# Gated cross-attention block on one Trainium2 core: fewer row maxima ahead of the first step, more inside group 0, and weight rounding 23 steps later

## The chip, the cores and the metric

One NeuronCore of one Trainium2 chip. The time is device microseconds for one launch of the kernel, the median of several runs.

## What is computed

The reference takes `x` (4 batches, 512 rows, 512 columns) and a context of 4 x 1601 x 512:

```python
x = x + tanh(g_xattn[0]) * attention(layernorm(x), ctx_2048, ctx_2048)   # 16 heads of 32, scores / sqrt(32)
x = x + tanh(g_ffn[0]) * ffn(layernorm(x))     # fp8-quantised weights and rows, I = 1408
# attention: scores masked to -10000 where key > query + (1601 - 512), softmax over keys, times values
# ffn: each weight row scaled by max|row| / 448 and rounded to fp8 e4m3, likewise each row of x and of the hidden layer
```

The softmax subtracts a shift that is the row maximum of the scores, so each head's scores are made twice: once (queries as rows) for the maxima and once (keys as rows) for the exponentials.

## The kernel before, in words

The work is 16 groups (`GALL`): 4 batches x 4 groups of 4 heads. A group is 26 **steps** (`STEPS` = 2 head pairs x 13 tiles of 128 keys), and every engine runs the same loop `for at in range(END)` with `gg, u = divmod(at, STEPS)`; what an engine does in a step is written out by hand. There is one queue of instructions for each engine, in order, and semaphores between them.

In each step of group `gg`:

- PE makes one **maximum job** (`max_turn`, L777: two matmuls of K = 32 into a slot of two PSUM banks, plus mask matmuls L782 on the diagonal) for a later group, then the two heads' scores (`scores`, L839), then the value product of two steps earlier (`values`, L863).
- DVE reduces the maximum job (`max_reduce`, L1066) out of its slot. There are two slots (banks 4-5 and 6-7), taken in turn by all short PSUM jobs: maximum, stage, suffix, shift, turned output and weight. PE waits for a slot until its job before last has been taken out.
- ACT makes the exponentials (`exps`, L629).

A group has 26 maximum jobs: 13 for its first head pair, 13 for its second. In each 13, the fifth to the eighth are narrower ones. Before, all 26 jobs of group 0 and the first 6 (`AHEAD`) of group 1 run before step 0; from then on there is one a step, always 6 steps ahead (`max_job_at`). After the last job of a group DVE makes `m16` (`max_finish`, L1068 to L1077), PE turns it (`shift_turn`, L791), ACT copies it to `mrow` (L605), and SP's queue sends it by DMA into the last row of `qst` (`put_shift`, L340). `scores` waits for that row (`mrow_in`) at step 0 of its group.

Each group's keys and queries are turned and split into high and low halves two groups ahead (`stage_turn` L764/L756, `stage_high` L589, `stage_low` L1057), and SP's queue copies them into `kst` and `qst` with 24 DMAs a group (`put_heads`, L335/L336).

The **SP queue** also issues nearly all loads, in program order. Ahead of step 0: `x`, keys of group 0, gates, index, keys of group 1, value tiles 0 to 2, the 24 `put_heads` DMAs of group 0, value tiles 3 to 12 (`load_values`, L321), `put_shift(0)` (L340), two down-weight loads (L326), keys of group 2, `put_heads` of group 1.

The **weights** are quantised in 26 jobs: 4 of 1408 columns (down weights, 7 steps apart), 22 of 512 (3 steps apart), starting at `weight_base(j)`. A job is DVE statistics (L996 to L1000), ACT scaling (L559, L562), DVE exponent, rounder and add (L978, L982, L986), a POOL subtraction (L416), PE transposes (L917, L919) and ACT copies (L570 to L577). The first row tile of the FFN starts at step 119 (`tile_base(0)`).

Every group also has three stage jobs at steps 10, 13, 19, a suffix job (L805 to L810, DVE L1082) at step 8, two outputs (`out_turn` L820, `join_out` L1096 to L1109) at steps 4 and 17, `max_finish` at step 20, and the shift at step 23. Every fourth group loads the next batch's values.

## Time and profile before

| what | before |
|---|---|
| median of 3 runs | 1157.04 us (1155.66 to 1158.47) |
| the profiled execution's own time | 1155.15 us |
| its span | 1153.4 us |
| PE busy | 969.0 us (84%) |
| DVE busy | 862.0 us (75%) |
| ACT busy | 656.3 us (57%) |
| POOL busy | 312.9 us (27%) |
| mean granted TensorE clock | 0.952 |

The profiled execution is 1.9 us below the median. Busy shares are averages over the whole span; for this change the stretch before the first scores and the groups 0 to 4 matter, so they are read by time below.

### The profile page before, as it was taken

The page shows a single profiled execution, that of the slowest core. Times are in us where ns is not written, and L with a number is a line of the kernel's source. Part 1 is how long each engine was busy: PE and PEld are TensorE (multiplying, and loading weights), DVE is VectorE, ACT ScalarE, POOL GpSimd, SP SyncE. Part 2 cuts the span into 40 slices and gives each one's busy share as a digit, 9 for nine tenths or more (in the row PEclk, how much of TensorE's full clock was granted, in tenths as well). Part 3 has the DMA queues.
Part 4 walks back from the last instruction along what each step waited for, and adds up shares of the span by engine and source line. Part 5 has one row for each costly group of instructions (what it writes and reads, how often), then busy time and mean ns, then how long its engine had stood idle before and what let it go on. Part 6 is the DMA issues. An engine that isn't in the chain of part 4 may idle for free.

```text
span 1153.4 us, 21093 instructions
## 1 busy us (share of the span) xinstructions
PE 969.0 (84%) x7770; PEld 399.7 (35%) x7770; DVE 862.0 (75%) x1450; ACT 656.3 (57%) x1343; POOL 312.9 (27%) x338
## 2 busy tenths in 40 slices
PE   4588889888879989999889999999889999983444
PEld 2233333333323333333334333333334343442222
DVE  7768789887747887777687878787778777436775
ACT  2165567676636666666556666666566666763322
POOL 3012334332101423232322232232323232433212
PEclk9998899999989999999999999999899999995766
DMA  7942423231572212124822221108621020000000
GB/s 149 159 118 67 117 67 94 66 78 35 103 98 53 71 47 49 44 53 71 125 46 63 67 55 41 48 24 128 81 56 40 20 48 11 2 10 10 10 10 19
DMA packets 155119, 70.69 MB, mean 61 GB/s; under 512 B 111032, under 2 KB 142856, under 8 KB 155016
## 3 DMA queue, kind: packets, MB, share of 16 engines
q1 hardware_dynamic: 153256, 63.57, 26.8%
q0 software_dynamic: 1760, 5.77, 1.8%
q8 instruction: 62, 1.02, 0.4%
q14 instruction: 41, 0.34, 0.1%
HBM read 39.08 MB, written 4.19 MB: 38 GB/s over the span
## 4 chain that ended last, share of the span: by engine, by line
PE 42%; DVE 38%; issue 11%; ACT 4%; POOL 3%; DMA 1%; SPq 0%; POOLq 0%; DVEq 0%; ACTq 0%
DVE mch L1066 18%; PE ps L863 12%; PE ps L839 8%; PE ps L884 6%; PE ps L777 5%; PE ps L907 3%; DVE ff L982 2%; DVE ff L978 2%; DVE ff L986 2%; PE ps L782 2%; ACT pr L629 1%; DVE upd L1109 1%; DMA qst<-mrow 1%; DVE cmb L1099 1%; PE ps L845 1%
## 5 line engine op out<-in xcount | busy, mean ns | idle before, releaser
L629 ACT ACTIVATE pr<-ps 128x512 f32<-128x512 f32 (+4 forms) x832 | 397.1, 530 | 247.0 <-PE ps L839 125.8
L1066 DVE TENSOR_REDUCE mch<-ps 128x2 f32<-128x1024 f32 (+4 forms) x416 | 432.0, 1055 | 68.2 <-PE ps L777 32.8
L863 PE MATMUL ps<-pr,vf 128*33 128x512 f32 (+4 forms) x1664 | 379.8, 536 | 0.0
L839 PE MATMUL ps<-qst,kst 97*64 97x512 f16 (+4 forms) x1600 | 250.6, 371 | 17.7 <-DMA qst<-mrow 11.2
L777 PE MATMUL ps<-kTh,qTh 32*128 32x512 f16 (+4 forms) x832 | 156.0, 373 | 60.0 <-DVE mch L1066 40.9
L777 PEld LDWEIGHTS ps<-kTh,qTh 32*128 32x128 f16 x832 | 39.5, 91 | 277.9 <-DVE mch L1066 106.9
L839 PEld LDWEIGHTS ps<-qst,kst 97*64 97x64 f16 (+1 forms) x1600 | 77.3, 111 | 107.3 <-ACT pr L629 57.1
L863 PEld LDWEIGHTS ps<-pr,vf 128*33 128x33 f32 (+1 forms) x1664 | 86.9, 113 | 57.1 <-issue 5.5
L1142 DVE SCALAR_TENSOR_TENSOR ff<-ps,scs,wsb 128x352 f32<-128x352 f32 x56 | 32.6, 583 | 71.3 <-PE ps L884 71.2
L884 PE MATMUL ps<-wgu,t_T 128*64 128x352 bf16 x768 | 66.5, 316 | 0.0
L445 POOL TENSOR_TENSOR t_q<-ff 128x768 bf16<-128x768 f32 (+1 forms) x24 | 40.4, 1682 | 87.5 <-DVE ff L986 87.5
L429 POOL TENSOR_TENSOR ff<-ff,wsb 128x352 f32<-128x352 f32 x48 | 45.9, 957 | 64.6 <-DVE ff L1142 64.6
L1057 DVE TENSOR_TENSOR kTl<-ps,kTh 128x1024 f16<-128x1024 f32 (+1 forms) x32 | 31.6, 991 | 40.7 <-ACT kTh L589 40.7
L845 PE MATMUL ps<-maskT,idb 128*64 128x128 bf16 (+2 forms) x576 | 61.4, 213 | 0.0
L450 POOL TENSOR_TENSOR xs<-xs,ff 128x512 f32<-128x512 f32 x14 | 17.8, 1272 | 143.9 <-DVE ff L1186 143.9
L986 DVE TENSOR_TENSOR ff<-ff 128x512 f32<-128x512 f32 (+3 forms) x66 | 55.0, 833 | 2.1
L656 ACT ACTIVATE ff<-ps,scs 128x352 f32<-128x352 f32 x48 | 26.6, 553 | 52.2 <-PE ps L884 52.2
L884 PEld LDWEIGHTS ps<-wgu,t_T 128*64 128x64 bf16 x768 | 44.4, 111 | 32.6 <-issue 20.8
L457 POOL TENSOR_TENSOR xs<-xs,upd 128x256 f32<-128x256 f32 x32 | 23.9, 748 | 107.9 <-DVE upd L1109 107.9
L433 POOL TENSOR_TENSOR ff<-ff 128x352 f32<-128x352 f32 x48 | 51.7, 1078 | 3.8
L486 POOL TENSOR_TENSOR cw<-w,count 128x16 f32<-128x16 f32 x16 | 3.9, 245 | 166.0 <-ACT w L612 166.0
L782 PE MATMUL ps<-idb,maskT 128*64 128x128 bf16 (+2 forms) x640 | 47.0, 229 | 0.0
(152 smaller groups left out, 1188.1 us busy)
## 6 DMA issues: line engine op xcount, KB each, us to landing
kst<-kTh SPq DMA_DIRECT2D x128, 100.1 KB, 2.2
ksrc<-in_ctx SPq DMA_DIRECT2D x16, 768.0 KB
vf<-in_ctx SPq DMA_DIRECT2D x48, 256.0 KB, 5.1
kst<-kTl SPq DMA_DIRECT2D x64, 100.1 KB, 2.2
xs<-in_x SPq DMA_DIRECT2D x16, 256.0 KB, 4.1
qst<-qTh SPq DMA_DIRECT2D x128, 32.0 KB, 1.9
out<-xs SPq DMA_DIRECT2D x16, 256.0 KB, 2.0
ff<-in_L_ffn_w_down SPq DMA_DIRECT2D x4, 704.0 KB, 4.9
```

The lines of the kernel that those rows point to most:

```text
L429: nc.gpsimd.tensor_tensor(t_u[e][:, cols], t_u[e][:, cols], wsb[:, I + c * CW:I + (c + 1) * CW], ALU.mult).then_inc(gated, 1)
L433: nc.gpsimd.tensor_tensor(t_u[e][:, cols], t_u[e][:, cols], t_g[e][:, cols], ALU.mult).then_inc(gu_ready, 1)
L445: nc.gpsimd.tensor_tensor(t_q[e][:, cols], t_v[e][:, cols], t_m[e][:, cols], ALU.subtract).then_inc(qt_ready, 1)
L629: nc.scalar.activation(pr[0:kn, n % NP, q0:S], ps[0:kn, j, q0:S], ACT.Exp, scale=SCALE).then_inc(ex_done, 1)
L777: last = nc.tensor.matmul(slot(job)[:, 512 * i:512 * i + k1 - k0], qTh[rows, gg % 2, qt * P:(qt + 1) * P], kTh[rows, gg % 2, k0:k1], start ...
L782: last = nc.tensor.matmul(slot(job)[a:e, 512 * i + lo - k0:512 * i + hi - k0], maskT[:, a:e], idb[:, lo - d0:hi - d0], start=False, stop=True)
L839: last = nc.tensor.matmul(ps[a:e, j, q0:S], kst[s][0:ST, r, k0 + a:k0 + e], qst[s][0:ST, r, q0:S], start=True, stop=(t < DT))
L845: last = nc.tensor.matmul(ps[a:e, j, q0:q0 + n_m], idb[:, a:e], maskT[:, m0:m0 + n_m], start=False, stop=True)
L863: nc.tensor.matmul(ps[64 * j:64 * j + VW, 2 + pp % 2, q0:S], vf[0:kn, t, h, :], pr[0:kn, n % NP, q0:S], start=(t == 0), stop=(t == NT - 1) ...
L884: last = nc.tensor.matmul(ps[a:e, bank(job) + side, 0:CW], qxT[:, k, a:e], wgu[:, k, side * I + c * CW:side * I + (c + 1) * CW], start=(k ...
L986: return nc.vector.tensor_tensor(v, v, m, ALU.add)
L1066: nc.vector.tensor_reduce(mch[:, qt, 2 * hp:2 * hp + 2, c], both[:, :, 0:k1 - k0], AX.X, ALU.max).then_inc(dve_free, 1)
```

## The change

Ahead of step 0 only the 13 jobs of group 0's first pair remain, followed by a shift for two heads (`first_finish`, `first_shift_turn`, `first_shift_copy`, `put_first_shift`). Group 0's other 13 jobs run in steps 0 to 7, group 1's 26 in steps 8 to 22, and the first 6 of group 2 in steps 23 to 25, so 45 jobs run in group 0 where 26 did. The second pair's shift is made at steps 8 to 10 and awaited at step 13. Group 1's `max_finish` and shift move to steps 23 and 24 (from 20 and 23), and group 0's suffix job from step 8 to 12. All weight jobs start 23 steps later. Smaller moves: the gate matmul and its Tanh come later in the prologue, the one-row memset of `kst[1]` goes from DVE to POOL, and POOL makes `rstd` ahead of both memsets; down-weight loads 2 and 3 are issued in group 1.

```diff
+    HALF = CH // PAIRS
+    FIRST = [(0, HALF + j) for j in range(HALF)] + [(1, j) for j in range(CH)] + [(2, j) for j in range(AHEAD)]
+    def first_until(at):
+        if at < 8:
+            return -(-HALF * (at + 1) // 8)
+        return HALF + -(-CH * (at - 7) // 15) if at < 23 else HALF + CH + 2 * (at - 22)
-    def max_job_at(at):
+    def max_jobs_at(at):
+        if at < STEPS:
+            return FIRST[first_until(at - 1) if at else 0:first_until(at)]
         gg, j = divmod(at + AHEAD, STEPS)
-        return (gg + 1, j) if gg + 1 < GALL else None
+        return [(gg + 1, j)] if gg + 1 < GALL else []
+    def finish_at(gg):
+        return FINISH_AT if gg else 23
+    def shift_at(gg):
+        return MT_AT if gg else 24
+    def suf_at(gg):
+        return SUF_AT if gg else 12
...
     def weight_base(j):
-        return 1 + 7 * j if j < DC else 1 + 7 * DC + 3 * (j - DC)
+        return 24 + (7 * j if j < DC else 7 * DC + 3 * (j - DC))
...
+        def put_first_shift(sp, i):
+            sp.wait_ge(act_free, act_count["shift", 0, i])
+            sp.dma_start(qst[0][ST - 1:ST, 2 * i:2 * i + 2, :], mrow[0:2, :]).then_inc(mrow_in[0], 16)
...
             for t in range(3, NT):
                 load_values(sp, 0, t)
-            put_shift(sp, 0)
+            put_first_shift(sp, 0)
...
                 if gg == 0:
+                    put_first_shift(sp, 1)
+                if g == 1 and b + 1 < B:
+                    load_x(sp, b + 1)
+                if gg == 1:
                     load_down(sp, 2)
                     load_down(sp, 3)
-                if g == 1 and b + 1 < B:
-                    load_x(sp, b + 1)
...
-            nc.gpsimd.memset(kst[0][ST - 1:ST, :, :], 1.0).then_inc(ones_in[0], 1)
-            pool.wait_ge(ones_in[0], 1)
             row_std(pool, 0)
-            masked_count(pool, 0)
+            pool.wait_ge(rstd_ready, 1)
+            for i in range(2):
+                nc.gpsimd.memset(kst[i][ST - 1:ST, :, :], 1.0).then_inc(ones_in[i], 1)
...
             if u == 0:
-                pe.wait_ge(mrow_in[s], (gg // 2 + 1) * 16)
+                pe.wait_ge(mrow_in[s], row_count(gg) if gg else 16)
+            if gg == 0 and u == NT:
+                pe.wait_ge(mrow_in[0], row_count(0))
...
-            pe.wait_ge(gin, 32)
-            nc.tensor.matmul(ps[:, 0, 0:2], onesf[0:1, :], gates[0:1, :], start=True, stop=True).then_inc(gate_mm, 1)
-            for part in PARTS:
-                stage_turn(pe, 0, part)
-            for j in range(CH):
+            stage_turn(pe, 0, PARTS[0])
+            stage_turn(pe, 0, PARTS[1])
+            pe.wait_ge(gin, 32)
+            nc.tensor.matmul(ps[:, 0, 0:2], onesf[0:1, :], gates[0:1, :], start=True, stop=True).then_inc(gate_mm, 1)
+            stage_turn(pe, 0, PARTS[2])
+            for j in range(HALF):
                 max_turn(pe, 0, j)
-            shift_turn(pe, 0)
+            first_shift_turn(pe, 0)
             for part in PARTS:
                 stage_turn(pe, 1, part)
-            for j in range(AHEAD):
-                max_turn(pe, 1, j)
...
-                if max_job_at(at) is not None:
-                    max_turn(pe, *max_job_at(at))
+                for job in max_jobs_at(at):
+                    max_turn(pe, *job)
+                if at == 9:
+                    first_shift_turn(pe, 1)
...
+        def first_finish(dve, s, i):
+            hs = slice(2 * i, 2 * i + 2)
+            dve.wait_ge(dve_free, dve_count["max", 0, HALF * (i + 1) - 1])
+            s.step(nc.vector.tensor_reduce(mg[:, :, hs], mch[:, :, hs, :], AX.X, ALU.max))
+            s.settle()
+            s.step(nc.vector.tensor_tensor(mg[:, :, hs], mg[:, :, hs], floor[:, :, hs], ALU.max))
+            s.settle()
+            nc.vector.tensor_scalar(m16[:, 0, :, hs], mg[:, :, hs], -1.0, None, ALU.mult).then_inc(m_ready, 1)
```

**How the order moves, PE, start of group 0.** The names: L777 is a maximum job (L820 after the change), L839 the scores (L892), L863 the value product (L916), L782 the mask (L825). Before, steps 0 to 3:

```order
L839 MATMUL ps<-qst0,kst0 64x512 x4
L777 MATMUL ps<-kTh,qTh 128x65 x2
L782 MATMUL ps<-idb,maskT 64x65 x4
L839 MATMUL ps<-qst0,kst0 64x512 x4
L777 MATMUL ps<-kTh,qTh 128x512 x2
L839 MATMUL ps<-qst0,kst0 64x512 x4
L863 MATMUL ps<-pr,vf 33x512 x2
L777 MATMUL ps<-kTh,qTh 128x512 x2
L839 MATMUL ps<-qst0,kst0 64x512 x4
L863 MATMUL ps<-pr,vf 33x512 x2
```

And steps 0 to 3 after it:

```order
L820 MATMUL ps<-kTh,qTh 128x512 x4
L892 MATMUL ps<-qst,kst 64x512 x4
L820 MATMUL ps<-kTh,qTh 128x512 x4
L892 MATMUL ps<-qst,kst 64x512 x4
L820 MATMUL ps<-kTh,qTh 128x449 x2
L825 MATMUL ps<-idb,maskT 64x128 x4
L892 MATMUL ps<-qst,kst 64x512 x4
L916 MATMUL ps<-pr,vf 33x512 x2
L820 MATMUL ps<-kTh,qTh 128x193 x2
L825 MATMUL ps<-idb,maskT 64x128 x4
```

A step now often has two maximum jobs (`128x512 x4`) ahead of its scores; of the 26 steps of group 0, 19 have two.

**DVE, around the third down-weight job.** Before, L986 is the last DVE part of that job, L1073 to L1077 is group 1's `max_finish`:

```order
L1066 TENSOR_REDUCE mch<-ps 128x2
L986 TENSOR_TENSOR ff<-ff 128x1408
L1073 TENSOR_REDUCE mg<-mch 128x16
L1075 TENSOR_TENSOR mg<-mg,floor 128x16
L1077 TENSOR_SCALAR m16<-mg 128x16
```

After, the first down-weight job, whose last DVE part is L1040, with the output of the pair before (L1159 to L1172) soon behind it:

```order
L1040 TENSOR_TENSOR ff<-ff 128x1408
L1120 TENSOR_REDUCE mch<-ps 128x2
L1159 TENSOR_TENSOR den<-cw,ps 128x4 x2
L1162 TENSOR_TENSOR cmb<-ps,sw 128x4x32 x2
L1167 RECIPROCAL den<-den 128x8
L1172 SCALAR_TENSOR_TENSOR upd<-cmb,tg,den 128x256
```

The weight jobs no longer run beside `max_finish` but beside the outputs of group 1.

## Rows read from the trace of the kernel before

**Rows 1.** Page: busy engines, and the chain that ended last by line.

```profile
PE 969.0 (84%) x7770; PEld 399.7 (35%) x7770; DVE 862.0 (75%) x1450; ACT 656.3 (57%) x1343; POOL 312.9 (27%) x338
DVE mch L1066 18%; PE ps L863 12%; PE ps L839 8%; PE ps L884 6%; PE ps L777 5%; PE ps L907 3%; DVE ff L982 2%; DVE ff L978 2%; DVE ff L986 2%; PE ps L782 2%; ACT pr L629 1%; DVE upd L1109 1%; DMA qst<-mrow 1%; DVE cmb L1099 1%; PE ps L845 1%
```

**Rows 2.** Chain in order of time, 0 to 66 us: start, length (us), what.

```profile
25.75 11.28 DVE mch L1066 x10
...
53.42 5.63 DVE mch L1066 x5
...
59.99 0.85 PE ps L839 x4
```

**Rows 3.** Timeline of SP's queue, 12 to 54 us: start, length, queue, line, DMA.

```profile
12.45 0.40 SPq L311 DMA_DIRECT2D ksrc<-in_ctx  x1
...
13.64 5.22 SPq L321 DMA_DIRECT2D vf<-in_ctx  x3
18.91 1.73 SPq L335 DMA_DIRECT2D kst<-kTh  x1
...
35.29 16.69 SPq L321 DMA_DIRECT2D vf<-in_ctx  x10
52.03 0.77 SPq L340 DMA_DIRECT2D qst<-mrow  x1
```

**Rows 4.** Timeline, 46 to 60 us: the shift's copy, first value sums, first scores.

```profile
46.66 0.57 ACT L605 COPY mrow<-ps 4x512 f16<-4x512 f16 x1 [28.22 <-PE ps L791]
55.52 0.29 POOL L479 COPY vsum<-vf 128x128 f32<-128x128 f32 x1 [7.78 <-DMA vf<-in_ctx]
59.78 1.06 PE L839 MATMUL ps<-qst,kst 97*64 97x512 f16 x4
```

**Rows 5.** Timeline, 0 to 16 us: what the prologue waits for.

```profile
9.00 0.55 PE L925 MATMUL ps<-gates,onesf 1*128 1x2 f32 x2 [9.00 <-DMA gates<-in_g_ffn]
9.48 2.93 PE L764 MATMUL ps<-idf,ksrc 128*128 128x128 f32 x13
```

**Rows 6.** Timeline of PE, two full steps of group 0 and one short one.

```profile
67.17 0.39 PE L777 MATMUL ps<-kTh,qTh 32*128 32x512 f16 x2
67.49 0.62 PE L839 MATMUL ps<-qst,kst 97*64 97x512 f16 x4
67.94 1.03 PE L863 MATMUL ps<-pr,vf 128*33 128x512 f32 x4
68.90 0.39 PE L777 MATMUL ps<-kTh,qTh 32*128 32x512 f16 x2
...
87.26 0.36 PE L777 MATMUL ps<-kTh,qTh 32*128 32x449 f16 x2 [1.06 <-DVE kTl L1057]
...
88.84 0.26 PE L777 MATMUL ps<-kTh,qTh 32*128 32x193 f16 x2
```

**Rows 7.** Timeline of DVE: the finish of group 0's maxima.

```profile
45.25 0.22 DVE L1073 TENSOR_REDUCE mg<-mch 128x16 f32<-128x64 f32 x1
45.50 0.17 DVE L1075 TENSOR_TENSOR mg<-mg,floor 128x16 f32<-128x16 f32 x1
45.71 0.17 DVE L1077 TENSOR_SCALAR m<-mg 128x16 f16<-128x16 f32 x1
```

**Rows 8.** Timeline, 113 to 130 us: third down-weight job, group 1's shift and scores.

```profile
113.04 3.16 POOL L416 TENSOR_TENSOR t_q<-ff 128x1408 bf16<-128x1408 f32 x1 [6.53 <-DVE ff L986]
113.13 3.11 DVE L1075 TENSOR_TENSOR mg<-mg,floor 128x16 f32<-128x16 f32 x1
117.84 1.39 PE L917 MATMUL ps<-idb,t_q 128*128 128x128 bf16 x11 [3.48 <-DVE mch L1066]
125.56 0.63 SPq L340 DMA_DIRECT2D qst<-mrow  x1
...
129.09 0.60 PE L839 MATMUL ps<-qst,kst 97*64 97x512 f16 x4
```

**Rows 9.** Timeline, 314 to 324 us: the shift row of group 4.

```profile
314.35 5.31 SPq L321 DMA_DIRECT2D vf<-in_ctx  x4
319.70 1.33 SPq L340 DMA_DIRECT2D qst<-mrow  x1
323.70 1.06 PE L839 MATMUL ps<-qst,kst 97*64 97x512 f16 x4 [5.55 <-DMA qst<-mrow]
```

**Rows 10.** Groups 0 to 4 (windows): us, busy by engine, granted clock, DMA, GB/s.

```profile
60.00:130.00 70.00, 59.62 (x410) 22.14 (x406) 53.07 (x63) 40.92 (x80) 12.56 (x7) 0.90 0.31 81
130.00:195.00 65.00, 55.99 (x432) 21.99 (x430) 53.95 (x102) 42.58 (x96) 25.20 (x24) 0.97 0.33 89
195.00:256.00 61.00, 53.67 (x421) 21.44 (x419) 52.42 (x97) 42.88 (x97) 21.47 (x23) 1.00 0.29 78
256.00:324.00 68.00, 53.94 (x413) 20.97 (x411) 47.11 (x82) 39.78 (x89) 13.72 (x16) 0.96 0.45 81
324.00:383.00 59.00, 54.99 (x417) 20.64 (x415) 39.37 (x65) 33.72 (x71) 8.44 (x12) 0.93 0.34 61
```

**Rows 11.** Timeline of PE, one step at the lower clock.

```profile
98.14 0.61 PE L777 MATMUL ps<-kTh,qTh 32*128 32x512 f16 x2
98.68 1.06 PE L839 MATMUL ps<-qst,kst 97*64 97x512 f16 x4
99.53 1.92 PE L863 MATMUL ps<-pr,vf 128*33 128x512 f32 x4
101.38 0.61 PE L777 MATMUL ps<-kTh,qTh 32*128 32x512 f16 x2
```

More of the change, by code:

```diff
@@ L144, in flamingo_gated_block @@
             numbered("turn", turned_at(at))
-        if gg < GALL and u == SUF_AT:
+        if gg < GALL and u == suf_at(gg):
             numbered("suf", gg)
-        if max_job_at(at) is not None:
-            numbered("max", *max_job_at(at))
-        if gg + 1 < GALL and u == MT_AT:
+        for job in max_jobs_at(at):
+            numbered("max", *job)
+        if at == 9:
+            numbered("shift", 0, 1)
+        if gg + 1 < GALL and u == shift_at(gg):
             numbered("shift", gg + 1)
@@ L532, in _ @@
                     row_std(pool, gg // NG + 1)
-                if gg + 1 < GALL and u == MT_AT:
+                if at == 10:
+                    masked_count(pool, 0)
+                if gg + 1 < GALL and u == shift_at(gg):
                     masked_count(pool, gg + 1)
@@ L599, in norm_cols, with first_shift_copy @@
                                      scale=rstd[:, qt:qt + 1]).then_inc(xl_ready, 1)
+        def first_shift_copy(act, i):
+            act.wait_ge(mT_mm, i + 1)
+            if i == 1:
+                act.wait_ge(mrow_in[0], 16)
+            nc.scalar.copy(mrow[0:2, :], slot(("shift", 0, i)).bitcast(f16)[0:2, 0:S]).then_inc(act_free, 1)
         def shift_copy(act, gg):
-            act.wait_ge(mT_mm, gg + 1)
-            if gg >= 1:
-                act.wait_ge(mrow_in[(gg - 1) % 2], ((gg - 1) // 2 + 1) * 16)
+            act.wait_ge(mT_mm, shift_count(gg))
+            act.wait_ge(mrow_in[(gg - 1) % 2], row_count(gg - 1))
             nc.scalar.copy(mrow[:, :], slot(("shift", gg)).bitcast(f16)[0:GH, 0:S]).then_inc(act_free, 1)
         def masked_weight(act, gg):
-            act.wait_ge(m_ready, gg + 1)
+            act.wait_ge(m_ready, shift_count(gg))
             if gg >= 2:
@@ L688, in _ @@
             act.wait_ge(consts, 15)
-            act.wait_ge(gate_mm, 1)
-            nc.scalar.activation(tg[:, :], ps[:, 0, 0:2], ACT.Tanh).then_inc(gate_th, 1)
             stage_high(act, 0, 1)
@@ L694, in _ @@
             stage_high(act, 0, 0)
+            act.wait_ge(gate_mm, 1)
+            nc.scalar.activation(tg[:, :], ps[:, 0, 0:2], ACT.Tanh).then_inc(gate_th, 1)
             norm_cols(act, 1, range(QT))
-            shift_copy(act, 0)
-            masked_weight(act, 0)
+            first_shift_copy(act, 0)
             for part in PARTS:
@@ L707, in _ @@
                     out_copy(act, turned_at(at + 2))
-                if gg + 1 < GALL and u == MT_AT:
+                if at == 9:
+                    first_shift_copy(act, 1)
+                    masked_weight(act, 0)
+                if gg + 1 < GALL and u == shift_at(gg):
                     shift_copy(act, gg + 1)
@@ L784, in max_turn, with first_shift_turn @@
             last.then_inc(mx_mm, 1)
+        def first_shift_turn(pe, i):
+            job = ("shift", 0, i)
+            free_slot(pe, job)
+            pe.wait_ge(m_ready, i + 1)
+            for qt in range(QT):
+                last = nc.tensor.transpose(slot(job).bitcast(f16)[0:2, qt * P:(qt + 1) * P], m16[:, 0, qt, 2 * i:2 * i + 2], idh[:, :])
+            last.then_inc(mT_mm, 1)
         def shift_turn(pe, gg):
@@ L941, in _ @@
                     out_turn(pe, turned_at(at))
-                if gg < GALL and u == SUF_AT:
+                if gg < GALL and u == suf_at(gg):
                     suffix_turn(pe, gg)
-                if max_job_at(at) is not None:
-                    max_turn(pe, *max_job_at(at))
-                if gg + 1 < GALL and u == MT_AT:
+                for job in max_jobs_at(at):
+                    max_turn(pe, *job)
+                if at == 9:
+                    first_shift_turn(pe, 1)
+                if gg + 1 < GALL and u == shift_at(gg):
                     shift_turn(pe, gg + 1)
@@ L1191, in _ @@
             nc.vector.memset(ps[:, 2:4, :], 0.0).then_inc(ps_clear, 1)
-            nc.vector.memset(kst[1][ST - 1:ST, :, :], 1.0).then_inc(ones_in[1], 1)
             dve.wait_ge(consts, 15)
@@ L1200, in _ @@
                 stage_low(dve, 0, part)
-            for j in range(CH):
+            for j in range(HALF):
                 max_reduce(dve, 0, j)
-            max_finish(dve, s, 0)
+            first_finish(dve, s, 0)
             for part in PARTS:
                 stage_low(dve, 1, part)
-            for j in range(AHEAD):
-                max_reduce(dve, 1, j)
             dve.wait_ge(gate_th, 1)
@@ L1210, in _ @@
                 gg, u = divmod(at, STEPS)
-                if gg + 1 < GALL and u == FINISH_AT:
+                if at == 8:
+                    first_finish(dve, s, 1)
+                if gg + 1 < GALL and u == finish_at(gg):
                     max_finish(dve, s, gg + 1)
@@ L1216, in _ @@
                     join_out(dve, s, turned_at(at))
-                if gg < GALL and u == SUF_AT:
+                if gg < GALL and u == suf_at(gg):
                     suffix_weigh(dve, gg)
-                if max_job_at(at) is not None:
-                    max_reduce(dve, *max_job_at(at))
+                for job in max_jobs_at(at):
+                    max_reduce(dve, *job)
                 if NG <= gg < GALL and gg % NG == 0:
```

18 lines of the change are left out of this document (11 added, 7 removed).

## Prediction

> **What bounds the kernel now.** The page comes first. It shows PE busy 84% and DVE 75%, and the largest share of the chain that ended last is the maximum reduction on DVE, 18% [rows 1]. Both are averages, so the second view is the chain in order of time. Before the first scores it is nearly nothing but DVE reducing maxima: ten reductions take 11.28 us, so one costs 1.13 us, and group 1's first jobs run at the same pace [rows 2]. That is the stretch from which the change takes work. The first scores start at 59.78 us [rows 4]; four steps later the picture is another one: a full step lasts 68.90 - 67.17 = 1.73 us and PE has no gap in it, 0.32 us for the maximum job, 0.45 for the scores, 0.96 for the values [rows 6]. Inside the groups PE sets the pace and one reduction of 1.13 us hides beside it; before them DVE does.
>
> The third view is SP's queue, because the first scores also need the shift row. The reader should see that the row's copy on ACT is done at 46.66 + 0.57 = 47.23 us [rows 4], but that SP issues its DMA only at 52.03: the queue is in the middle of ten value loads which take 16.69 us, 1.67 each [rows 3]. The last value tile has landed by 55.52, when POOL's first sum, which waited for it, starts [rows 4]. Before the change this costs nothing, as PE comes for the row at 59.78.
>
> **The change part by part.**
>
> *A. Fewer maxima ahead of step 0.* Removed are 13 jobs of group 0 and 6 of group 1; one more is then made in step 0 ahead of its scores (two instead of one). By the pace of rows 2 PE would reach the first scores 18 x 1.13 = 20.3 us earlier, at about 39.5. But the shift row stays behind the same ten value loads in SP's queue; the change doesn't move it. These loads follow the 24 copies of group 0's heads and the first three value loads, back to back from 13.64 us, and the queue has no pause that the shorter prologue could take away [rows 3]. So PE is let go when the row lands. No row shows its landing. Below it is bounded by its issue at 52.03, above by 4.00 us from issue to scores, which the row of group 4 needed, also behind value loads (323.70 - 319.70) [rows 9]: 52.0 to 56.0. I take 55.5, where the last value tile, just ahead of it on the queue, has landed. The queue itself can start a little earlier: it waits for PE's key transposes at 9.48 + 2.93 = 12.41, which began right behind the gate matmul [rows 5]; that matmul is now behind them, for which I give 0.1 us. **Gain 59.78 - 55.4 = 4.4 us** (3.8 to 7.8). The other edits of the prologue (memset from DVE to POOL, `rstd` earlier, Tanh later) only bring forward work that will now wait for the row anyway: nothing, covered by some 15 us of idle PE and DVE. If the row came early, they would be worth about one us.
>
> The Trainium skill, "DMA: Bandwidth & Descriptors", section "Queues, rings and completion order", says that descriptors of a ring are consumed in order but that completion is not first in, first out for the issuing engine. By it a small row can finish before the big loads ahead of it; the gain would rise towards the 7.8 us of the early bound. The issue time is not touched by that rule.
>
> *B. More maxima in group 0.* Behind the first scores group 0 now has 43 jobs instead of 25, so 18 more. Floor: PE's own 0.32 us each, 5.8 us, since PE has no gap in a full step. Ceiling: 18 whole reductions, 20.3 us. Between them, two reductions take 2.26 us and a full step with two jobs needs 1.73 + 0.32 = 2.05 of PE, so a step with two jobs behind another such step runs at DVE's pace, +0.53, and one behind a step with a single job at PE's, +0.32. By `first_until` ten are of the first sort and eight of the second: 10 x 0.53 + 8 x 0.32 = 7.9. Five of them are steps at the ends of a pair with narrower scores, 1.58 us long [rows 6], which DVE's 2.26 stretches further: together +1. The second finish (0.22 + 0.17 + 0.17 on DVE [rows 7]) and its four transposes add 0.5, and stage and suffix work on DVE, so far beside PE, now partly counts, 0.6. **Cost 10.0 us** (5.8 to 14; nearest to PE's price, as DVE is full only in every second step or so).
>
> *C. Group 1's shift.* It is turned in step 24 instead of 23. Before, 129.09 - 125.56 = 3.5 us lie between the row's issue and the next group's first scores [rows 8], with one step more. Group 0's last steps now last about 2.3 us instead of 1.6, which gives back most of it. **Cost 0.3 us** (0 to 1.5). Nothing waits behind it on SP but copies for group 2. On SP the second pair's row, issued in step 9 and awaited in step 13, stands ahead of the keys of group 3, which wait for the stage job at step 13 anyway: nothing.
>
> *D. Weights 23 steps later.* The same 26 jobs, with the same instructions, now lie in steps 24 to 119. Group 0 loses its three and a half (four with the tail), group 4 gets some five. The stretches of groups 0 to 4 show what jobs cost: 65 and 61 us with weights, 59 without, but with the first row tile [rows 10]; nothing says that a job is cheaper in group 4 than in group 0. Two places differ. In group 0 the 3.16 us subtraction on POOL met `max_finish`: a 16-column operation took 3.11 instead of 0.17 us, and PE idled 3.48 [rows 7, 8]. That meeting ends, worth up to 117.84 - 116.20 = 1.6 us. In its place the subtractions of the first and third jobs meet the outputs at steps 30 and 43. And the 5.55 us for which PE waits at the start of group 4 [rows 9] shrink a little, as weights now fill the steps ahead, perhaps 0.7. Against that the last jobs lie beside layer-norm statistics in group 4. **Gain 0.5 us** (from 4 gained to 3 lost). What is late next is the first row tile: it starts in step 119, one step behind the last POOL subtraction.
>
> The Trainium skill, "SBUF — State Buffer", section "SBUF: two separate sides", says that a DVE operation with two SBUF inputs and a GpSimd operation that reads SBUF exclude each other for a whole instruction. The 3.11 us row agrees with it, and the rule speaks against this change: `upd` has two SBUF inputs. By it, term D would be a loss of up to 3 us instead of a gain of 0.5.
>
> **Sum:** -4.4 + 10.0 + 0.3 - 0.5 = +5.4 us. On the profiled execution's 1155.15 us that makes 1160.6. The median of the runs lies 1.9 us above that execution, and the same difference on 1157.04 gives 1162.4; I forecast **1162.5 us, slower**. The row that the shorter prologue no longer waits for on DVE, it now waits for on DMA, and the moved maxima are paid again inside group 0.
>
> **The rivals.**
>
> *The queue lets go early, so it is faster.* The mechanism: the ten value loads take 1.67 us each only because nobody needs them sooner, and the row goes out with PE. Then PE starts at about 40 us, a gain of 19.5 to 20, and the time is 1157.04 - 20 + 10 = 1147. It decides once the row lands before about 48 us. Against it: SP is never free between 35.29 and 52.03 [rows 3], and the edit doesn't reorder it. For it only that no row shows the landing. Chance 0.06.
>
> *The clock gives it back.* A mean clock of 0.90 over group 0's 70 us means 14 us at the lower level, 1.2 GHz, where a step lasts 101.38 - 98.14 = 3.24 instead of 1.73 us [rows 10, 11]. The fall came behind PE's waits in the weight jobs, of which 3.48 us is the longest [rows 8]. If group 0 without weights stays at 2.4 GHz and group 1 with them does too, up to 14 x (1 - 1.73 / 3.24) = 6.5 us are gained: 1156. I count nothing, since the same waits come along with the jobs. Chance 0.20, of which 0.06 with a result that is faster.
>
> *The outputs are held by POOL,* as said under D, at steps 30 and 43, each at most 3.11 us and in part beside PE's own wait for the same subtraction: some 3 us on top, 1165.5. For it the row of 3.11 us; against it that `upd` comes late in its step. It decides where POOL's subtraction starts within about 3 us ahead of `upd`. Chance 0.14.
>
> *DVE is the bound in all of group 0.* Each pair of slots holds PE up, the reductions come one after another and nothing hides: 15 us or more in B, and 1167 to 1173. For it, 43 reductions of at most 1.13 are 48 us and the rest of DVE's work some 6; against it that group 0 is longer than that. Chance 0.07.
>
> **How the numbers follow.** The forecast's own case has 0.53, with 1159 to 1166 as its own range. From 1155 to 1169 the range also takes most of the clock's case and of POOL's, and leaves out the early queue (0.06), the worst of the DVE case and a tail of the clock. A measurement of this kernel can tell 0.2%, 2.3 us, from no change. Faster: 0.06 from the queue and 0.06 from the clock, 0.12. Same: 0.14 from the clock and 0.06 of the forecast with B near its floor, 0.20. Slower: the rest, 0.68.
>
> **What would show it.** Right: the first scores at 55 to 56 us with an idle time of some 15 us ended by the DMA of `qst<-mrow`; SP's row for it at about 52; group 0 some 63 us from its first scores (129.09 - 59.78 = 69.3, less three and a half down-weight jobs at 3.16 + 1.39 us [rows 8], plus 10); no lower clock in it behind the first steps; then groups 1 to 3 with weight waits as groups 0 to 2 had, and a small DVE operation of about 3 us beside a subtraction on POOL if the third rival holds. Wrong: first scores near 40 us (A), group 0 under 60 or over 70 us (B), a mean clock of 1.00 in group 1 (the clock), or groups 1 to 4 together longer than their 253 us [rows 10] by far more or less than the 16 us of weights that moved into them (D).

## The result and the profile after

| what | before | after |
|---|---|---|
| median of the runs | 1157.67 us (5 runs) | 1166.43 us (5 runs, 1164.67 to 1169.83) |
| ratio, with its 95% interval | | 1.0085 [1.0062, 1.0108] |
| the profiled execution's own time | 1155.15 us | 1165.79 us |
| its span | 1153.4 us | 1164.0 us |
| mean granted TensorE clock | 0.952 | 0.942 |

The change makes the kernel slower by 0.85%, some 9.8 us by the ratio (the two medians lie 8.8 apart). The forecast was 5.4 us slower, so the sign and the range held and the size was short by 4.4 us. The two profiled executions differ by 10.6 us, close to that, so their traces can be laid side by side.

The page first, busy engines and the chain that ended last. This answers to [rows 1]:

```profile
PE 973.3 (84%) x7774; PEld 400.5 (34%) x7774; DVE 858.5 (74%) x1452; ACT 656.5 (56%) x1344; POOL 319.1 (27%) x339
DVE mch L1120 16%; PE ps L916 13%; PE ps L892 8%; PE ps L937 6%; PE ps L820 5%; PE ps L960 3%; DVE ff L1036 2%; PE ps L825 2%; SPq L347 2%; DVE ff L1032 2%; DVE ff L1040 1%; DMA qst<-mrow 1%; DVE upd L1172 1%; ACT pr L670 1%; DVE cmb L1162 1%
```

The reductions lost 2 points of the chain and the ten value loads on SP's queue (L347) are in it with 2%: the start now hangs on them. The averages say nothing more, so again the view is by time. In all windows below, the numbers behind the length are the busy us of PE, PE's weight load, DVE, ACT and POOL, then the granted clock, DMA's share and GB/s. The timeline of SP's queue, 34 to 54 us, with PE's and POOL's first instructions behind it, answers to [rows 3, 4]:

```profile
34.99 16.58 SPq L347 DMA_DIRECT2D vf<-in_ctx  x10
51.63 0.85 SPq L366 DMA_DIRECT2D qst<-mrow  x1
...
54.98 1.06 PE L892 MATMUL ps<-qst,kst 97*64 97x512 f16 x4 [14.33 <-DMA qst<-mrow]
55.28 0.29 POOL L511 COPY vsum<-vf 128x128 f32<-128x128 f32 x1 [35.12 <-DMA vf<-in_ctx]
```

PE stands idle for 14.33 us and is let go by the row's DMA, at 54.98 instead of 59.78. Then the groups, as windows from first scores to first scores, to be read against [rows 10]. First before and after for group 0 alone, then groups 1 to 4 after:

```profile
59.78:129.09 69.31, 58.93 (x404) 21.94 (x402) 52.17 (x62) 40.44 (x79) 12.56 (x7) 0.90 0.31 81
```

```profile
55.00:129.00 74.00, 65.28 (x431) 21.29 (x433) 50.71 (x62) 31.78 (x66) 2.30 (x6) 0.87 0.28 73
129.00:197.00 68.00, 59.19 (x433) 23.47 (x435) 56.83 (x77) 40.56 (x81) 21.43 (x15) 0.90 0.32 87
197.00:260.00 63.00, 57.36 (x423) 21.96 (x421) 51.98 (x97) 42.77 (x98) 21.08 (x22) 0.93 0.26 73
260.00:326.00 66.00, 53.76 (x421) 21.32 (x415) 54.23 (x100) 43.24 (x97) 22.89 (x24) 0.99 0.54 110
326.00:393.00 67.00, 60.19 (x447) 24.28 (x449) 49.53 (x91) 42.08 (x92) 15.24 (x17) 0.90 0.29 57
```

Group 0 (54.98 to 129.12) is 4.8 us longer than before, although it has lost its weight jobs: POOL's 12.56 us have become 2.30. Groups 1 to 4 take 264 us where they took 253. From group 5 on the two executions take the same time. So the 10.6 us are: 4.8 gained ahead of the first scores, 4.8 lost in group 0, 10.6 lost in groups 1 to 4. Read by terms it is another sum, since the weights leave group 0 and enter the others; that separation needs the experiments.

### The profile page after: what moved, and what is told of

Its sections match the earlier page's. It is cut to its first block, busy times and chain, and to the rows that moved or that the text cites. A ratio compares the mean times of both kernels' runs of the same rounds, so it can differ in the third digit from the quotient of the medians.

```text
span 1164.0 us, 21109 instructions
## 1 busy us (share of the span) xinstructions
PE 973.3 (84%) x7774; PEld 400.5 (34%) x7774; DVE 858.5 (74%) x1452; ACT 656.5 (56%) x1344; POOL 319.1 (27%) x339
## 4 chain that ended last, share of the span: by engine, by line
PE 43%; DVE 35%; issue 10%; ACT 4%; SPq 3%; POOL 2%; DMA 2%; DVEq 0%; POOLq 0%; ACTq 0%
DVE mch L1120 16%; PE ps L916 13%; PE ps L892 8%; PE ps L937 6%; PE ps L820 5%; PE ps L960 3%; DVE ff L1036 2%; PE ps L825 2%; SPq L347 2%; DVE ff L1032 2%; DVE ff L1040 1%; DMA qst<-mrow 1%; DVE upd L1172 1%; ACT pr L670 1%; DVE cmb L1162 1%
## 5 line engine op out<-in xcount | busy, mean ns | idle before, releaser
L916 PE MATMUL ps<-pr,vf 128*33 128x512 f32 (+4 forms) x1664 | 384.7, 543 | 0.0
L892 PE MATMUL ps<-qst,kst 97*64 97x512 f16 (+4 forms) x1600 | 253.4, 376 | 31.5 <-DMA qst<-mrow 25.2
L820 PE MATMUL ps<-kTh,qTh 32*128 32x512 f16 (+4 forms) x832 | 153.6, 369 | 56.1 <-DVE mch L1120 35.0
L820 PEld LDWEIGHTS ps<-kTh,qTh 32*128 32x128 f16 x832 | 39.0, 91 | 273.1 <-DVE mch L1120 102.4
L892 PEld LDWEIGHTS ps<-qst,kst 97*64 97x64 f16 (+1 forms) x1600 | 77.9, 112 | 122.2 <-ACT pr L670 55.8
L916 PEld LDWEIGHTS ps<-pr,vf 128*33 128x33 f32 (+1 forms) x1664 | 87.9, 114 | 58.9 <-issue 8.2
L1040 DVE TENSOR_TENSOR ff<-ff 128x512 f32<-128x512 f32 (+3 forms) x66 | 55.0, 833 | 2.1
L825 PE MATMUL ps<-idb,maskT 128*64 128x128 bf16 (+2 forms) x640 | 47.3, 230 | 0.0
```

Source lines behind the costliest of these rows:

```text
L820: last = nc.tensor.matmul(slot(job)[:, 512 * i:512 * i + k1 - k0], qTh[rows, gg % 2, qt * P:(qt + 1) * P], kTh[rows, gg % 2, k0:k1], start ...
L825: last = nc.tensor.matmul(slot(job)[a:e, 512 * i + lo - k0:512 * i + hi - k0], maskT[:, a:e], idb[:, lo - d0:hi - d0], start=False, stop=True)
L892: last = nc.tensor.matmul(ps[a:e, j, q0:S], kst[s][0:ST, r, k0 + a:k0 + e], qst[s][0:ST, r, q0:S], start=True, stop=(t < DT))
L916: nc.tensor.matmul(ps[64 * j:64 * j + VW, 2 + pp % 2, q0:S], vf[0:kn, t, h, :], pr[0:kn, n % NP, q0:S], start=(t == 0), stop=(t == NT - 1) ...
L1040: return nc.vector.tensor_tensor(v, v, m, ALU.add)
```

## The experiments

All ratios are to the kernel before, run on the same chip.

**The weights alone.** The kernel before with nothing but the later weight base and the two loads that follow it:

```diff
-        return 1 + 7 * j if j < DC else 1 + 7 * DC + 3 * (j - DC)
+        return 24 + (7 * j if j < DC else 7 * DC + 3 * (j - DC))
```

> The kernel before with the weight jobs alone moved 23 steps later (and down-weight loads 2 and 3 issued in group 1, without which the queue would wait for itself). My term D: the same jobs cost the same elsewhere, 0.5 us gained, so a ratio of 0.996 to 1.003 to the kernel before; group 0 falls from 69.3 us between first scores to some 54, groups 1 to 4 together rise from 253 to some 268. Rival: the weights are what makes the changed kernel slow, since they now lie beside outputs and layer-norm statistics and pull the clock down there; then this kernel alone is 4 us or more slower, ratio 1.004 or above.

Measured: 1151.68 us in 12 runs, 0.9945 [0.9925, 0.9965]: faster by 6.4 us (4.1 to 8.7). This half of the change is a gain, and it was costed at 0.5. Its windows, groups 0 to 4:

```profile
59.33:110.98 51.65, 50.57 (x365) 17.31 (x363) 32.99 (x39) 29.47 (x62) 0.94 (x2) 0.92 0.30 73
110.98:178.95 67.97, 57.68 (x430) 22.22 (x430) 56.16 (x79) 40.87 (x81) 20.17 (x14) 0.92 0.30 85
178.95:240.54 61.59, 54.57 (x427) 21.38 (x424) 52.01 (x96) 43.44 (x97) 22.02 (x23) 1.00 0.28 77
240.54:306.94 66.40, 54.12 (x426) 21.54 (x423) 54.37 (x100) 43.61 (x99) 22.88 (x24) 0.99 0.55 110
306.94:378.86 71.92, 66.15 (x447) 25.52 (x448) 49.89 (x91) 42.38 (x92) 15.22 (x17) 0.82 0.27 53
```

The five groups take 319.5 us against 322.6 from first scores to first scores before (59.78 to 382.38). PE is busy 5 us longer in them (283.1 against 277.8; the clock of the last is 0.82) but idle some 8 us less (36.4 against 44.8), and that is all group 0: 10.4 idle before, 1.1 now. The same jobs made PE wait more in group 0 than they do at the other end. Group 0 alone falls from 69.3 to 51.7 us, and the groups 1 to 4 rise from 253.3 to 267.9.

**The maxima alone.** The kernel after with the old weight base:

> The changed kernel with the weight jobs at their old steps (first at step 1), that is the moved maxima alone. If the two parts add, this is as much slower than the changed kernel as the kernel before is slower than e1, 6 us: ratio to the kernel before 1.012 to 1.016. If weights and a second maximum job meet on DVE in group 0 (54 us of weights-free work there plus some 20), group 0 becomes DVE-bound, 85 us or more, and the ratio is 1.018 or above: then moving the weights away is what makes the moved maxima bearable, and the parts do not add.

Measured: 1172.08 us, 1.0118 [1.0096, 1.0139]. The maxima without the weights' move cost 13.7 us, the start's gain already taken off. Group 0 takes 88.0 us here (55.83 to 143.85), as long as the second case of the expectation had it, but DVE is busy only 66.8 of them, so DVE does not fill it, and the ratio lies at the foot of the first case. With the two halves done alone at 1.0118 and 0.9945, adding them gives 1.0063 where both together give 1.0085; the difference lies within the intervals. So the late weights are worth 6.4 us when they move alone and 3.8 us (1.0118 to 1.0085) beside the moved maxima, and these data don't tell the two apart.

**The row ahead of the value loads.** After, with `put_first_shift(sp, 0)` in front of the ten loads:

```diff
+            put_first_shift(sp, 0)
             for t in range(3, NT):
                 load_values(sp, 0, t)
-            put_first_shift(sp, 0)
```

> The changed kernel with the first shift row issued ahead of value tiles 3 to 12 on SP's queue. Theory A (the value loads hold the row and PE idles 14.33 us for it): the row is issued at about 35 us, right behind the head copies, the first scores start at about 41 us, and the whole kernel is 12 to 14 us shorter than the changed one, about 1153, ratio to the kernel before 0.995 to 0.998. Rival: the value tiles, now later by the row's microsecond, or the heads of group 1 set the next wait, and most of the 14 us comes back inside group 0; then 1160 or more, ratio above 1.001.

Measured: 1157.49 us, 0.9988 [0.9964, 1.0012], some 11 us less than after. SP's queue and PE's timeline:

```profile
35.12 0.67 SPq L366 DMA_DIRECT2D qst<-mrow  x1
35.84 16.44 SPq L347 DMA_DIRECT2D vf<-in_ctx  x10
...
40.34 1.06 PE L892 MATMUL ps<-qst,kst 97*64 97x512 f16 x4
```

PE comes to the scores at 40.34 and waits for nothing. This is the 39.5 us that the pace of the reductions gave under A; the queue alone was holding it to 55. Of the 14.6 us that the start came forward, 3 or 4 did not arrive at the end (the expectation had 12 to 14 arriving): group 0 takes 75.5 us here, 1.3 more than after, and where the rest went was not followed.

**The second job behind the scores.** After, with a step's second maximum job, and the shifts of group 0, issued on PE between the scores and the value product instead of ahead of the scores:

```diff
-                for job in max_jobs_at(at):
+                for job in max_jobs_at(at)[:1]:
...
+                for job in max_jobs_at(at)[1:]:
+                    max_turn(pe, *job)
```

> The changed kernel with PE making the second maximum job of a step behind the step's scores instead of ahead of them (the shift transposes of group 0 move along). Theory S: group 0 is 11 us longer than I summed because with two jobs ahead of the scores PE waits for a slot with nothing else to do, above all where a stage job holds the other slot (PE transposes, ACT cast, DVE subtraction, then the second job: waits of 1.83 and 1.21 us); then group 0 falls from 74 to about 70 us and the kernel is 3 to 5 us shorter than the changed one. Rival: DVE and the lower clock set group 0's length, not the place of the wait; then no change within 1.5 us.

Measured: 1163.25 us, 1.0052 [1.0029, 1.0075], 3.8 us less than after by the ratios, whose intervals overlap. Group 0, first scores to first scores:

```profile
55.80:123.60 67.80, 61.02 (x431) 19.10 (x431) 51.49 (x63) 31.70 (x65) 2.31 (x6) 0.91 0.30 79
```

It is 6 us shorter with the same jobs and the same 51 us of DVE. So DVE is not full in group 0. Of the 6 us only some 2 are less waiting (PE is idle 6.8 us, 8.7 in the kernel after); the other 4 are the same matmuls taking less time, because less of the group runs at the lower clock level: behind the first steps one stretch of 3.4 us (95.6 to 99.0), where the kernel after has four, 18.9 us in all. The wait behind the stage job is still there, and here it is not followed by the lower level (timeline of PE; compare the fences under "Filling the waits"):

```profile
82.96 0.26 PE L820 MATMUL ps<-kTh,qTh 32*128 32x193 f16 x2 [1.44 <-DVE kTl L1115]
...
83.28 1.02 PE L916 MATMUL ps<-pr,vf 128*33 128x512 f32 x4
```

**Both together.**

> Both edits together. If A and S are separate terms the two gains add: 15 to 19 us below the changed kernel, 1148 to 1152, ratio to the kernel before 0.991 to 0.995, a version faster than both. If the second job's wait only mattered because of what the idle time ahead of the first scores does to the clock, the sum is no better than the row's edit alone, about 1153.

Measured: 1151.19 us, 0.9936 [0.9909, 0.9963]. That is 17 us below after, and the two edits alone gave 11.2 and 3.8: the gains add, within the intervals. Row first, second job behind the scores: the whole change becomes a gain, though no larger than the late weights alone (0.9945). In other words, moving nineteen maxima has by then stopped costing anything, and has not begun to gain.

**Filling the waits.** After, with 30 matmuls of 512 columns (the expectation says 27) into a bank that nothing reads, each lot just ahead of a place where PE waited for a slot in group 0 (steps 9, 10, 12, 13, 14, 24). They compute nothing that is used:

```diff
+        FILL = {9: 3, 10: 8, 12: 2, 13: 5, 14: 3, 24: 3}
...
+                nc.tensor.matmul(ps[:, 3 if at < 15 else 2, :], qTh[0:HD, 1, 0:P], kTh[0:HD, 1, 0:512], start=True, stop=True)
```

> The changed kernel with 27 extra matmuls of 512 columns in group 0, written to a bank that holds nothing then, at the places where PE waits for a slot (steps 9, 10, 12, 13, 14, 24). They give nothing but work for PE while it would wait. Clock theory: of the 21 us that group 0 is longer than with the same weights and one job a step (e1: 53.3 us, here 74.1), about 6 are the lower clock that follows these waits (19.7 us of it here against 7.2 in e1, at 0.47 us each); with the waits filled group 0 falls to some 68 to 70 us and its mean clock rises from 0.87 to 0.93 or more, and the kernel is 3 to 6 us shorter than the changed one. Rival: the clock falls for another reason and the extra work only adds to the queue; then the kernel is the same or up to 3 us longer, at the same clock.

Measured: 1161.38 us, 1.0034 [1.0015, 1.0053]. That is 5.9 us less than after, by adding work. Group 0, windows as above, and the fill beside the wait of step 10 (timeline of PE; L978 is the fill):

```profile
55.37:122.05 66.68, 63.80 (x465) 21.86 (x466) 50.31 (x62) 31.55 (x66) 2.30 (x6) 1.00 0.30 80
```

```profile
79.36 1.90 PE L978 MATMUL ps<-kTh,qTh 32*128 32x512 f16 x8
81.26 0.26 PE L820 MATMUL ps<-kTh,qTh 32*128 32x193 f16 x2
```

The same place in the kernel after, timeline of PE, ACT and DVE:

```profile
79.13 1.19 PE L807 MATMUL ps<-idf,ksrc 128*128 128x128 f32 x8
80.25 0.36 PE L820 MATMUL ps<-kTh,qTh 32*128 32x449 f16 x2
80.36 1.01 ACT L625 CAST kTh<-ps 128x1024 f16<-128x1024 f32 x1 [1.23 <-PE ps L807]
81.40 1.22 DVE L1111 TENSOR_TENSOR kTl<-ps,kTh 128x1024 f16<-128x1024 f32 x1 [4.47 <-ACT kTh L625]
82.68 0.28 PE L820 MATMUL ps<-kTh,qTh 32*128 32x193 f16 x2 [1.83 <-DVE kTl L1111]
...
83.87 1.91 PE L916 MATMUL ps<-pr,vf 128*33 128x512 f32 x4
```

A stage job (L807) takes one slot and the step's first maximum job the other. The second maximum job has to wait until ACT and then DVE have taken the stage job out, 1.83 us in which PE has nothing else it may do, as its scores stand behind that job. Then the value product, 1.03 us elsewhere, takes 1.91: TensorE is at its lower level. With the wait filled it stays at the upper one, the granted clock of the whole group is 1.00 instead of 0.87, and group 0 is 7.5 us shorter. The fills themselves keep PE busy for 7.8 us, so the kernel's own matmuls take 63.8 - 7.8 = 56.0 us instead of 65.4, while waiting and filling together take 10.7 us instead of 8.7. So the gain is the clock's.

One thing in these clocks misleads. The group's first matmuls, up to 61.3 us, last as long as at the lower level in both kernels (scores 1.06, a value product 1.91), but the column says 1.00 for them:

```profile
54.98:61.30 6.32, 6.32 (x26) 1.38 (x26) 3.37 (x3) 3.26 (x6) 1.14 (x3) 1.00 1.09 338
59.49 1.91 PE L916 MATMUL ps<-pr,vf 128*33 128x512 f32 x4
```

With the late weights alone the same kind of stretch (59.33 to 66.4) is in the column with 0.50. So the group's 0.87 leaves the start out and the 0.92 of the late weights is nearly all start. The expectation set these two side by side, 19.7 us of the lower clock against 7.2. Behind the start it is 18.9 us against none, and at 0.47 us each that is an estimate of 8.9 us, where the expectation had about 6.

**One operation on DVE moved off POOL's subtraction.** The late weights alone brought a new meeting, which the timeline shows in group 1; in the second fence the same two instructions with the variance (L1022) made a step earlier:

```profile
155.22 3.15 POOL L416 TENSOR_TENSOR t_q<-ff 128x1408 bf16<-128x1408 f32 x1
156.03 2.36 DVE L1022 TENSOR_SCALAR ve<-mv 128x4 f32<-128x4 f32 x1
158.52 0.80 PE L917 MATMUL ps<-idb,t_q 128*128 128x128 bf16 x11 [2.83 <-POOL t_q L416]
```

```profile
153.49 0.17 DVE L1022 TENSOR_SCALAR ve<-mv 128x4 f32<-128x4 f32 x1
157.12 3.15 POOL L416 TENSOR_TENSOR t_q<-ff 128x1408 bf16<-128x1408 f32 x1
160.42 0.75 PE L917 MATMUL ps<-idb,t_q 128*128 128x128 bf16 x10 [2.84 <-POOL t_q L416]
```

```diff
-                if gg < GALL - NG and gg % NG == 1 and u == 17:
+                if gg < GALL - NG and gg % NG == 1 and u == (16 if gg == 1 else 17):
```

> e1 with the layer-norm variance of batch 1 made in step 42 instead of 43. In e1 and in the changed kernel its last operation (128x4, 0.17 us) lasts 2.36 us beside POOL's subtraction of the third down-weight job, and the step lasts 8 us. If it is held by POOL, as the 3.11 us operation of the kernel before was, it takes 0.17 us here, that step is 2 to 3 us shorter, and the kernel is 1.5 to 3 us below e1 (ratio 0.992 to 0.9935). Rival: PE waits for the same subtraction anyway, so the operation falls to 0.17 us and the step stays near 8 us: ratio as e1, 0.9945.

Measured: 1152.34 us, 0.9944 [0.9923, 0.9964], the same as the late weights alone. The operation is short again and nothing is gained: PE waits 2.8 us for the subtraction itself in both. That fits the second reading of the expectation.

**Six jobs moved instead of nineteen.** Late weights, all of group 0's maxima ahead of step 0, only the six of group 1 moved behind it (two jobs in steps 4, 5 and 15 to 18, none of them in a step of a stage job), the first pair's row ahead of the value loads, the second pair's at step 2:

```diff
-    FIRST = [(0, HALF + j) for j in range(HALF)] + [(1, j) for j in range(CH)] + [(2, j) for j in range(AHEAD)]
+    FIRST = [(1, j) for j in range(CH)] + [(2, j) for j in range(AHEAD)]
...
+        return at + 1 + sum(1 for two in (4, 5, 15, 16, 17, 18) if two <= at)
```

> Weights late as in e1, but only 6 maximum jobs moved: the 26 of group 0 stay ahead of step 0 (with the first pair's shift row sent ahead of the value tiles, the second pair's made in step 2), and the two-job steps of group 0 are six (4, 5, 15 to 18), none with a stage or suffix job, the second job behind the scores. Slot theory: a job moved into a step without stage or suffix job costs 0.3 to 0.5 us against 1.13 ahead of step 0, so this kernel is 3 to 4.5 us below e1, ratio to the kernel before 0.990 to 0.992. Rival: every moved job costs about its whole reduction (the 18 of the changed kernel cost 21 us, 1.16 each), so nothing is gained over e1: 0.994 to 0.995.

Measured: 1150.74 us, 0.9930 [0.9911, 0.9949]. Window of group 0; in the late weights alone, above, it was 51.65 us:

```profile
52.72:108.04 55.32, 53.42 (x391) 17.50 (x391) 39.66 (x49) 30.14 (x64) 2.24 (x6) 0.94 0.44 106
```

Six jobs cost 3.7 us, 0.61 each, and bring the first scores from 59.33 to 52.72, 1.1 each. In the kernel after, 18 jobs turned group 0 from 51.7 into 74.1 us, 1.25 each, and with the second job behind the scores, as here, into 68.0 us, 0.91 each. (The expectations take group 0 with late weights as 53.3 us, to 112.60. The next group's first scores start at 110.98, so 53.3 is 1.6 too long, and their 21 us and 1.16 a job are too small.) The gain over the late weights alone, some 1.7 us, is within the intervals, below the 3 to 4.5 that the slot theory gave and above the rival's nothing: the time of the whole kernel does not decide between them.

**Fills where they matter.** The six-job version, and the kernel before, each with some 35 unused matmuls of 256 columns (f32) ahead of the transposes of two down-weight jobs and of the first scores of groups 4, 8 and 12:

```diff
+        def fill(bank, n):
+            for _ in range(n):
+                nc.tensor.matmul(ps[0:64, bank, 0:2 * P], onesf[:, 0:64], later[:, :, :].rearrange("p a n -> p (a n)"), start=True, stop=True)
...
+                if gg in (4, 8, 12) and u == 0:
+                    fill(2, 8)
```

> e6 (weights late, six jobs moved) with 34 extra matmuls of 256 columns in f32 in PE's longest waits behind group 0: ahead of the transposes of the third and fourth down-weight job (waits of 2.84 and 1.85 us in e6) and ahead of the first scores of groups 4, 8 and 12 (3.94 and 3.47 us). Clock theory: the lower clock of groups 1 to 4 (34 us of it in e6) follows these waits too; with them filled at least 15 us of it go, at up to 0.47 us each, and the kernel is 3 to 7 us below e6, ratio to the kernel before 0.987 to 0.990. Rival: outside group 0 the clock falls for other waits, or the extra work reaches past the end of the waits; then the ratio is 0.992 to 0.995 as e6 or a little worse.

> The kernel before with such fillings alone: ahead of the transposes of its second and third down-weight job (waits of 1.71 and 3.48 us) and of the first scores of groups 4, 8, 12. Clock theory: the two stretches at the lower clock in group 0 (13.7 us) and the one at group 4 vanish at least in part, and the kernel is 3 to 6 us shorter, ratio 0.995 to 0.9975. Rival: no change, 0.999 to 1.001.

Measured: 1146.13 us for the first, 0.9899 [0.9863, 0.9935], and 1154.11 for the second, 0.9973 [0.9953, 0.9992]. The first has the lowest ratio of all versions. Groups 1 and 4 of the six-job version, first without them, then with:

```profile
109.42:177.72 68.30, 57.64 (x412) 21.59 (x414) 54.83 (x76) 39.96 (x81) 20.35 (x14) 0.90 0.30 84
...
304.66:373.44 68.78, 62.43 (x445) 24.34 (x447) 49.49 (x91) 42.22 (x92) 15.24 (x17) 0.87 0.30 58
```

```profile
110.40:176.77 66.37, 58.22 (x432) 23.67 (x434) 54.79 (x76) 40.05 (x81) 20.65 (x14) 0.97 0.31 86
...
304.99:371.26 66.27, 59.31 (x445) 24.16 (x447) 49.48 (x91) 42.43 (x92) 15.30 (x17) 0.92 0.30 57
```

(The windows of group 1 begin 1.4 us behind its first scores, in both.) The granted clock rises where the fills are, from 0.90 to 0.97 and from 0.87 to 0.92, and these groups are 1.9 and 2.5 us shorter. In group 0, which has no fill of its own, the column also goes from 0.94 to 1.00, but that is again the start: its first scores last 1.06 us and its first value product 1.92 in both, with 0.50 in the column in one and 1.00 in the other, and behind the start neither has a stretch at the lower level. The two ratios, 0.0031 apart or 3.6 us, have intervals that overlap, so of the two the clock is shown and the time is not. On the kernel before the interval stops just short of no change.

## Why the prediction was right, and where it was wrong

**A, the start: right.** The first scores came at 54.98, predicted 55.4; the wait was 14.33 us and the row's DMA ended it, SP's row stood at 51.63. The gain was 4.8 us for 4.4. Its bounds, 52.0 to 56.0, held. That the row arrived ahead of the last value tile (POOL's first sum at 55.28 still waited for that tile) is the 0.4 us between, and what the completion rule of the Trainium skill ("DMA: Bandwidth & Descriptors", section "Queues, rings and completion order") allowed for; the issue time behind the loads decided the rest. The rival in which the queue lets go early fell; putting the row first did what that rival described, and was worth 11 us.

**B, the maxima in group 0: right sign, less than half the size. This is the step that failed.** It was 10.0 us (5.8 to 14). By the traces it is 74.14 - 51.65 = 22.5 us, group 0 after against group 0 with late weights alone, which holds the same weights and 18 jobs fewer. By the prediction's own signs that is B wrong (group 0 over 70 us), and its "no lower clock behind the first steps" failed too. The view that splits it is the groups of PE in that window, first after, then the late weights alone:

```profile
L916 PE MATMUL ps<-pr,vf 128*33 128x512 f32 (+4 forms) x96 | 27.6, 661 | 0.0
L892 PE MATMUL ps<-qst,kst 97*64 97x512 f16 (+4 forms) x100 | 18.3, 436 | 14.3 <-DMA qst<-mrow 14.3
L820 PE MATMUL ps<-kTh,qTh 32*128 32x512 f16 (+4 forms) x88 | 16.8, 403 | 7.2 <-DVE mch L1120 3.2 <-DVE kTl L1111 3.0 <-DVE sw L1145 0.5
L825 PE MATMUL ps<-idb,maskT 128*64 128x128 bf16 (+2 forms) x70 | 5.9, 254 | 0.0
```

```profile
L863 PE MATMUL ps<-pr,vf 128*33 128x512 f32 (+4 forms) x96 | 23.9, 578 | 0.0
L839 PE MATMUL ps<-qst,kst 97*64 97x512 f16 (+4 forms) x100 | 16.9, 402 | 0.1
L777 PE MATMUL ps<-kTh,qTh 32*128 32x512 f16 (+4 forms) x52 | 9.7, 371 | 1.0 <-DVE kTl L1057 1.0
...
L782 PE MATMUL ps<-idb,maskT 128*64 128x128 bf16 (+2 forms) x44 | 3.3, 235 | 0.0
```

Three things were left out of the pace of 0.32 to 0.53 us a job:

- *The masks.* The jobs cost PE 7.1 us in L820, but their mask matmuls L825 another 2.6. The full step of [rows 6] from which the price was read has no mask.
- *The waits for a slot.* PE is idle 74.1 - 65.4 = 8.7 us in group 0, against 51.7 - 50.6 = 1.1. A steady pace of two reductions a step was the model; but PE waits 7.2 us ahead of L820, 3.0 of it for `kTl`: both slots are taken at a stage job, and the step's scores are queued behind the second maximum job. Step 10's wait of 1.83 us is the longest. Issuing that job behind the scores took 6 us off group 0, 2 of them waiting and 4 clock.
- *The clock.* The value products and scores, the same ones, last 661 and 436 ns instead of 578 and 402. Four stretches of 3.4 to 6.8 us behind such waits (at 76.0, 82.8, 96.4 and 123.8 us, 18.9 us of them in the group) have a granted clock of 0.50, which is the lower level, 1.2 GHz. Two of them here; PE is busy throughout:

```profile
82.80:86.20 3.40, 3.40 (x22) 1.18 (x22) 1.29 (x2) 0.81 (x2) 0.00 (x0) 0.50 0.00 0
96.40:103.20 6.80, 6.80 (x32) 1.90 (x34) 4.51 (x4) 3.13 (x7) 0.00 (x0) 0.50 0.08 18
```

With the waits filled group 0 took 66.7 us, which leaves 66.7 - 51.7 = 15.0 us for B. So 7.5 of the 22.5 us went with the clock, which the forecast had put at nothing, and what is left is still above the 14 of its range: masks and waits for a slot were missing in it as well. A small slip beside them: of the 18 steps with two jobs eleven, not ten, follow another such step, which adds 0.2 us.

**C, group 1's shift a step later:** 0.3 us predicted, none found. PE enters group 1's scores with no wait for the row. (Its transposes, though, had to wait 0.74 us for a slot at 123.17, ahead of the last of the four stretches; that is counted under B.)

**D, the weights later: the second wrong size,** 0.5 us predicted (4 gained to 3 lost), 6.4 measured (4.1 to 8.7). The step said that nothing shows a job to be cheaper in group 4 than in group 0. A hint was in [rows 10]: PE is idle 10.4 us in group 0 of before but 4.0 in group 4, and the jobs moved out took 9.3 idle us of group 0 with them and put 1.8 into group 4. Why a job is hidden better there was not separated; the cause of this gain stays open. In the profiled executions it is smaller, 3.1 us over groups 0 to 4, and the profiled one was the slowest of its twelve runs. Beside the moved maxima it was 3.8 us.

The two errors pull against each other. By the sum's own steps: -4.8 + 21.0 + 0 - 6.4 = +9.8, where the 21.0 is only what the other terms leave for B. The traces add up by another split: 4.4 us earlier first scores than with the late weights alone, 22.5 us in group 0, 4.0 us less in groups 1 to 4, and 3.5 us for the late weights, which is the 10.6 between the two profiled executions. In both, B is more than twice its forecast. That the time fell inside the stated range was in part luck: B was some 11 us too small and D some 6, and the two errors cancel in half.

**The rivals.** *The clock gives it back* (0.20) went the other way: group 1's clock is 0.90, not 1.00, and group 0's fell from 0.90 to 0.87. I had counted the lower clock as something that comes with weight jobs; it also comes behind waits for a slot, of which group 0 now has some ten. Not behind every one: in the kernel after those of 0.40 to 0.51 us between 105 and 116 us were not followed by it, nor was the 1.44 us with the second job behind the scores, nor one of 1.64 us at 75.87 in the kernel before. Which waits it follows was not found. *Outputs held by POOL* (0.14): the meeting is there, in the timeline behind the first weight job,

```profile
134.97 3.17 POOL L448 TENSOR_TENSOR t_q<-ff 128x1408 bf16<-128x1408 f32 x1 [9.61 <-DVE ff L1040]
136.78 1.64 DVE L1172 SCALAR_TENSOR_TENSOR upd<-cmb,tg,den 128x256 f32<-128x256 f32 x1
138.28 0.82 PE L970 MATMUL ps<-idb,t_q 128*128 128x128 bf16 x11 [0.40 <-POOL t_q L448]
```

where `upd` takes 1.64 us instead of some 0.49 and ends 0.3 us behind the subtraction. The rule of the Trainium skill cited under D ("SBUF — State Buffer", section "SBUF: two separate sides") holds for it. Its price looks wrong: the 3 us were to be lost on top, but PE waits for the subtraction's result in the same step anyway. What was tested is another operation, the variance `ve`, which suffered more: moving it away changed nothing in the time. `upd` itself was not moved. *DVE is the bound in all of group 0* (0.07) gave the size, 15 us or more in B, and not the reason: DVE is busy 50.7 of 74.1 us, and with the same DVE work group 0 takes 66.7 when PE's waits are filled.

## What to carry to other kernels

Work moved out of a stretch with one bound into a stretch with another is not paid at the busy time of either engine there: look at which buffer it takes, who holds that buffer at each step of the new place, and what is queued behind the wait. Six jobs put in steps with a free slot cost 0.61 us each, eighteen spread evenly 1.25, or 0.91 with the second job behind the scores. And before a start is shortened, read the queue that delivers its last input; here one DMA issued sixteen microseconds earlier gave 11 us, more than the 9.8 that the whole change had lost.
